# Feed-forward stage: the 3x3 convolution reads whole padded rows (464 columns) in place of 8 rows of 56 (448 columns)

## What is computed

```
y = _layer_norm(x, ln2_g, ln2_b)
y = conv(y, w_ffn1, 3x3, 'SAME')        # 48 -> 192 channels
y = gelu(y * bn1_scale + bn1_shift)     # exact gelu
y = conv(y, w_ffn2, 1x1)                # 192 -> 48 channels
return x + (y * bn2_scale + bn2_shift)
```

## Time and profile before

| | |
|---|---|
| median of 3 runs | 4128.19 us (4124.6 to 4130.14) |
| span of the profiled execution | 4125.0 us |
| last stage in that span | 2763 to 4120 us, nearly |
| TensorE busy over the span | 3958.8 us, 96% |
| matmuls in the last stage | 6272, of which 4928 in `convolve` |

### The profile page before, as it was taken

One profiled execution on the slowest core, in us unless ns is written; L12 is line 12 of the kernel. 1 busy time (PEld: TensorE's weight loads), 2 busy tenths in 40 slices (PEclk: granted clock), 3 DMA queues, 4 the chain that ended last, 5 costly groups with the idle time before them and its releaser, 6 DMA issues. The chain is left out here.

```text
span 4125.0 us, 76120 instructions
## 1 busy us (share of the span) xinstructions
PE 3958.8 (96%) x23156; PEld 2953.8 (72%) x23156; DVE 2712.5 (66%) x5076; ACT 2451.7 (59%) x4724; POOL 2335.8 (57%) x2216
## 2 busy tenths in 40 slices
PE   7888799999999999999999999969999999999999
PEld 3555577777777777777777777747777777777776
DVE  4454388888888888888888888854444444444443
ACT  3333177777777777777777777744444444444444
POOL 1111266666666666666666666635656565656554
PEclk8888799999999999999999999979999999999999
DMA  4331201111111111111111111125454545454442
GB/s 101 94 94 47 59 20 27 27 26 25 26 27 27 27 27 27 27 26 26 27 27 27 26 25 27 27 52 91 72 95 73 94 74 91 77 87 80 85 83 45
DMA packets 219355, 210.38 MB, mean 51 GB/s; under 512 B 113968, under 2 KB 214320, under 8 KB 216240
## 3 DMA queue, kind: packets, MB, share of 16 engines
q1 hardware_dynamic: 219312, 209.86, 25.1%
HBM read 132.00 MB, written 77.76 MB: 51 GB/s over the span
## 5 line engine op out<-in xcount | busy, mean ns | idle before, releaser
L1222 POOL TENSOR_TENSOR hid_lo<-hid,hid_hi 96x448 fp32r<-96x448 f32 x448 | 770.7, 1725 | 583.2 <-ACT hid_hi L1295 583.1
L590 POOL TENSOR_TENSOR kex<-ks,cw 112x294 f32<-112x294 f32 x1024 | 727.6, 745 | 88.2 <-ACT ks L852 88.2
L1292 ACT ACTIVATE hid<-ps_h,cw 96x448 f32<-96x448 f32 x448 | 323.6, 722 | 728.4 <-PE ps_h L1243 728.4
L683 PEld LDWEIGHTS ps_o<-pt,vex 98*118 98x118 f32 x6144 | 695.1, 183 | 56.4 <-ACT pt L882 2.6
L683 PE MATMUL ps_o<-pt,vex 98*118 98x118 f32 x6144 | 727.0, 268 | 0.5 <-ACT pt L882 0.5
L1354 DVE SCALAR_TENSOR_TENSOR xr<-ps_f,cw,xr 48x448 f32<-48x448 f32 x224 | 151.3, 676 | 773.7 <-PE ps_f L1254 773.7
L656 PE MATMUL ps_s<-kex,qbd 112*98 112x294 f32 x2048 | 592.0, 411 | 0.0
L1239 PE MATMUL ps_h<-ya_hi,wa_hi 128*96 128x448 f32 x1344 | 501.4, 373 | 28.8 <-DVE yb_sp L1328 28.8
L1239 PE MATMUL ps_h<-ya_hi,wa_lo 128*96 128x448 f32 x1344 | 498.6, 371 | 0.0
L1239 PE MATMUL ps_h<-ya_lo,wa_hi 128*96 128x448 f32 x1344 | 498.3, 371 | 0.0
L1015 DVE TENSOR_TENSOR s<-s,mx 98x588 f32<-98x588 f32 x512 | 466.5, 911 | 17.5
(11 more groups left out here) (153 smaller groups left out, 7081.4 us busy)
## 6 DMA issues: line engine op xcount, KB each, us to landing
ya<-y_chunks SPq DMA_DIRECT2D x64, 532.9 KB, 6.9
y_chunks<-y SPq DMA_DIRECT2D x256, 76.1 KB, 1.8
xin<-x_chunks SPq DMA_DIRECT2D x256, 73.5 KB, 2.5
x_chunks<-xo SPq DMA_DIRECT2D x256, 73.5 KB, 1.8
out<-xr SPq DMA_DIRECT2D x32, 588.0 KB, 8.2
yb<-y_chunks SPq DMA_DIRECT2D x96, 177.6 KB, 8.2
xr<-x_chunks SPq DMA_DIRECT2D x32, 514.5 KB, 5.5
xt<-x SPq DMA_DIRECT2D x16, 840.0 KB, 17.2
```

The lines of the kernel that those rows point to most:

```text
L590: pool.tensor_tensor(kex[a][:, win, :, :], ks[:, win, :].unsqueeze(1).to_broadcast([PP, HEADS, N]), w("head").unsqueeze(2).to_broadcast([P ...
L683: mm = pe.matmul(ps_o[0:OP, (win % 4) * OP:(win % 4 + 1) * OP], vex[a][:, win, j, 0:OP], pt[d % 2][:, start:start + OP], start=j == 0, sto ...
L1222: pool.tensor_tensor(hid_lo[:, U % slots, :], hid[:, U % slots, :], hid_hi[:, U % slots, :], ALU.subtract).then_inc(hid_lo_set, 1)
L1292: act.activation(hid[:, U % slots, :], ps_h[U % slots][0:half, 0:T1], ACT.Gelu, bias=w("t1")[:, U % 2:U % 2 + 1], scale=w("s1")[:, U % 2:U ...
```

## The change

`convolve` reads, for each matmul, one contiguous run of `TC = 8 * 58 = 464` numbers that starts at `c * TC + kw`. The run goes over the two pad numbers between rows, so it gives 464 results, and the last two of each 58 are of no use. They are written to `ps_h` too (464 of the bank's 512 numbers). The gelu of line 1292 reads `ps_h` as 8 rows of 56, 58 apart, and writes 448 contiguous numbers as before. A run with `kw` = 2 of the last tile ends two numbers behind the image, so `ya_hi` and `ya_lo` get two numbers more, which VectorE sets to zero once at the stage's start, and `first` takes two numbers more. `yb_sp` is read with `kw` = 0 alone and keeps its size.

```diff
+TC = R1 * YW
@@
-        ya_hi = [sb(f"ya_hi{a}", [128, H * YW], F32R) for a in range(2)]
-        ya_lo = [sb(f"ya_lo{a}", [128, H * YW], F32R) for a in range(2)]
+        ya_hi = [sb(f"ya_hi{a}", [128, H * YW + 2], F32R) for a in range(2)]
+        ya_lo = [sb(f"ya_lo{a}", [128, H * YW + 2], F32R) for a in range(2)]
@@
                 def pixels(tile, kw):
-                    return tile.rearrange("q (r n) -> q r n", r=H)[:, rows, kw:kw + W]
+                    return tile[:, c * TC + kw:(c + 1) * TC + kw]
@@
-                        pe.matmul(ps_h[bank][0:half, 0:T1], by_column(weights)[:, kw, hidden],
+                        pe.matmul(ps_h[bank][0:half, 0:TC], by_column(weights)[:, kw, hidden],
@@
-                    act.activation(hid[:, U % slots, :], ps_h[U % slots][0:half, 0:T1], ACT.Gelu,
+                    act.activation(hid[:, U % slots, :].rearrange("q (r n) -> q r n", r=R1),
+                                   ps_h[U % slots][0:half, 0:TC].rearrange("q (r n) -> q r n", r=R1)[:, :, 0:W], ACT.Gelu,
@@
             dve.memset(yb[:, (H - 1) * YW - 2:], 0.0)
+            for a in range(2):
+                dve.memset(ya_hi[a][:, H * YW:].bitcast(F32), 0.0)
+                dve.memset(ya_lo[a][:, H * YW:].bitcast(F32), 0.0)
@@
-            first, others = slice(0, first_rows * YW), slice(first_rows * YW, H * YW)
+            first, others = slice(0, first_rows * YW + 2), slice(first_rows * YW + 2, H * YW)
```

More of the change, by code:

```diff
@@ L1230, in convolve @@
             def convolve(bank, a, c, k):
-                rows = slice(c * R1, (c + 1) * R1)
                 hidden = slice(k * half, (k + 1) * half)
                 def pixels(tile, kw):
-                    return tile.rearrange("q (r n) -> q r n", r=H)[:, rows, kw:kw + W]
+                    return tile[:, c * TC + kw:(c + 1) * TC + kw]
                 for kw in range(3):
                     for i, (weights, image) in enumerate(((wa_hi, ya_hi), (wa_hi, ya_lo), (wa_lo, ya_hi))):
-                        pe.matmul(ps_h[bank][0:half, 0:T1], by_column(weights)[:, kw, hidden],
+                        pe.matmul(ps_h[bank][0:half, 0:TC], by_column(weights)[:, kw, hidden],
                                   pixels(image[a][:, :], kw), start=kw == 0 and i == 0, stop=False)
-                pe.matmul(ps_h[bank][0:half, 0:T1], wb_hi[:, hidden], pixels(yb_sp[a][:, :], 0), start=False, stop=False)
-                pe.matmul(ps_h[bank][0:half, 0:T1], wb_lo[:, hidden], pixels(yb_sp[a][:, :], 0),
+                pe.matmul(ps_h[bank][0:half, 0:TC], wb_hi[:, hidden], pixels(yb_sp[a][:, :], 0), start=False, stop=False)
+                pe.matmul(ps_h[bank][0:half, 0:TC], wb_lo[:, hidden], pixels(yb_sp[a][:, :], 0),
                           start=False, stop=True).then_inc(h_mm, 1)
```

## The result

The changed kernel takes 4139.15 us as the median of 7 runs (4132.41 to 4142.56), against 4127.84 us for the kernel before (7 runs, 4124.6 to 4130.6): 11.3 us more, a ratio of 1.0027 with a 95% interval of 1.0016 to 1.0038. The forecast was 4132 us. So it is slower, by a little more than the 0.2% that the prediction took as the bound of a wash, and that bound lies within the interval.

What follows compares the result with a forecast made beforehand. TensorE's matmuls were taken to bound the last stage. Terms +3.9 (matmuls), +0.15 (slow-clock start) and -0.3 us (waits) gave +3.8, a span of 4128.8, plus 3.2 around it: 4132 us, range 4120 to 4145.

Steps and rivals of the forecast that it cites:

- the wash: In `convolve`, 16 columns cost what the breaks cost, -0.8 to +1.7 ns a matmul; 4124 to 4136 us; chance 0.62.
- the slower case: Contiguous reads in `convolve` cost 205.3 ns plus 6.7 to 7.3 for columns; 4142 to 4145 us; chance 0.22.
- the prediction's own sign: Distance of matmul starts in `convolve` under 207.5 or over 211 ns would mean breaks or columns were priced wrongly.
- What bounds the kernel: TensorE, busy 96% of the span; the last stage lasts as long as its 6272 matmuls, 4928 of them changed.
- Removed: the breaks: Dropping the breaks between 8 rows of 56 in `convolve`'s operand takes a matmul from 209.2 to 203.3 ns.
- The step of 6.7 ns: First-stage price of stepping 8 rows of 56: stepped matmuls 210.0 ns each, contiguous ones behind them 203.3.
- Added: 16 columns at 6.7 ns: Each `convolve` matmul streams 16 more columns at 2.4 GHz, 6.7 ns, or 7.3 if the whole cost grows with columns.
- The sum for a matmul, +0.8 ns: In `convolve`, 203.3 + 6.7 = 210.0 ns against 209.2 now; over 4928 matmuls +3.9 us.
- a bound with a gain: Odd starts (`kw` = 1) may pay for each row now, only once later; 0.8 ns a matmul allowed, -3.9 us.
- ScalarE, the memsets, the waits, the slow clock: Last stage: gelu's pieces 0, memsets 0, shorter waits for `hid_lo` -0.3 us, first matmuls at 1.2 GHz +0.15 us.
- The page against the row: Skill page says non-contiguous PSUM access slows matmuls significantly; profile rows give 3% for a stepped operand; rows were followed.
- Both faster cases: Dearer breaks in `convolve`, 4120 us, chance 0.09; or unbroken runs at the column clock, 193.3 ns, 4050 us, chance 0.03.

Runs made afterwards that it cites:

- run448: Kernel before, but each matmul of `convolve` reads 448 contiguous numbers in place of 8 rows of 56, so pixels are wrong; 4103.52 us, ratio 0.9944.
- shifted: Against the kernel before: y stored three times, shifted by 0, 1, 2, without pads; vertical taps read 448 contiguous numbers at whole-row offsets; 4105.15 us, ratio 0.9951.
- after_kw0: Changed kernel with all nine matmuls over `ya` starting at offset 0, so the three taps read the same columns; 4132.36 us, ratio 1.0013.
- after_kw1: Changed kernel with all nine matmuls over `ya` starting at offset 1, so the three taps read the same columns; 4149.80 us, ratio 1.0056.
- before_kw1: Kernel before, 8 rows of 56, with all nine matmuls over `ya` at offset 1, so every row starts odd; 4131.03 us, ratio 1.0013.

## Why the prediction was right, and where its size was off

The time came out in the stated range, but the likeliest case did not come. 4139.15 us lies between the wash (to 4136) and the slower case (from 4142); it is in the range because that reached to both neighbours, and in this the number had luck. The forecast had the direction right and a third of the size, +3.8 us for +11.3. By the prediction's own sign, a distance over 211 ns, the pricing of a matmul was wrong: 211.6 ns was measured, and the last stage grew by 11 us where 2 to 6 were expected.

*What bounds the kernel.* Right. The loss is 2.4 ns on each of 4928 matmuls, 11.8 us, and the trace shows +11.0 us between the last stage's first and last matmul; medians say +11.3.

*Removed: the breaks.* Mis-sized. The sum took 203.3 ns for a contiguous 448, from line 293. That line's reads start at multiples of 448 only. The step of 6.7 ns was taken as a place "where all else is equal", but the stepped matmuls of line 282 have 128 weight columns and those of line 293 have 96. run448 measured 203.8 over the three offsets: the breaks gave back 5.4 ns, from 209.2.

*Added: 16 columns at 6.7 ns.* Right at offset 0 (6.9), too small on average (7.8): the odd offset pays 8.2, offset 2 pays 8.3, and `yb` 8.1 at offset 0.

*The sum for a matmul, +0.8 ns.* This is the term that was off, +2.4 measured. Two runs in which every start is a multiple of 8 numbers show what it left out: 448 contiguous columns cost 203.3 ns in shifted and 464 cost 210.1 in after_kw0, 6.8 ns apart, close to the clock's 6.7. So 203.3 + 6.7 = 210.0 ns holds for such starts, and the offsets 1 and 2 of the changed kernel add 1.5 ns (211.6), a cost for which the sum had no term. For the starts it had offered "a bound with a gain", that an odd start may be paid for each row now and only once later. after_kw0, after_kw1 and before_kw1 show the reverse: it is the contiguous read that pays for the odd start. From offset 0 to offset 1 for all nine matmuls the changed kernel goes from 210.1 to 214.2 ns, while the stepped one at offset 1 is 1.2 ns over its own mix. With every start at offset 0 the changed kernel takes the forecast time (4132.36 us measured; 4132 forecast).

*ScalarE, the memsets, the waits, the slow clock.* Right: 723 against 722 ns, no later start, 19.4 us of waits against 20.4, and 386 ns at 1.2 GHz.

*The page against the row.* The rows decided rightly. The Trainium skill, TensorE: Matmul & The Clock Gate, section Back-to-back issue gap, gives N / 2.4 + 2.5 ns for an isolated matmul. As an estimate that is 195.8 ns for 464 columns, and 211.6 was measured. For a stream of weight loads and matmuls, which this kernel is, the section has still less, some 131 ns at 512 columns; the traces don't agree with that either, since 448 contiguous columns take 203.3 ns in shifted.

*The rivals.* "Slower" gave 4142 to 4145 us for +2.8 to +3.4 ns, and it decides from +1.7 ns on; with +2.4 ns the outcome is on its side of the line, below its numbers. It named the odd starts as unknown, but put the price on all contiguous reads; that is wrong for offset 0. Both faster cases fell.

## What to carry to other kernels

Price a change of an access pattern by what it adds and what it removes in the same unit: here the breaks between 8 rows (5.4 ns) against 16 more columns (7.8 ns), and neither could be seen in a busy share of 96%. Where a matmul's operand is read from several offsets, take the cost for each offset, because a row from elsewhere in the trace has only its own. The gain lay in having neither: with the taps that need odd offsets put in the partitions by the stores, and the others as whole rows, the kernel reads 448 contiguous numbers and is 0.5% faster than before, at 4105.15 us.

## What the runs showed of the hardware that was not expected

- At 2.4 GHz a contiguous fp32r matmul whose operand starts at offset 1 costs 2.3 ns (448 columns), 2.7 (456) and 3.6 ns (464) more than one at offset 0, a multiple of 8 numbers into its tile, in the same kernel. At the same place in the run of 11, between after_kw0 and after_kw1, it is 3.7 to 6.2 ns (464). In a stepped read of 8 rows of 56 the difference is 0.7 ns in the trace of before and 1.0 at the same place (before_kw1). Every odd start here was one number behind a multiple of 8; others were not tried, and neither was why.
- A stepped PSUM output and a stepped PSUM read by ScalarE cost nothing for 8 rows of 56 (209.3 ns, 723 ns, against 209.2 and 722).
- The last two of 464 columns cost 1.5 ns, the two before them 0.3, where the clock gives 0.8 for either. Why was not settled.
- 448 contiguous columns at 2.4 GHz take some 203 ns, 16 more than 448 / 2.4 = 186.7; at 1.2 GHz 464 take 386 ns and nothing more. What the 16 ns are was not tried.
